# A fused two-layer block: biases in feature 0's row, three blocks of the Gram matrix, bank values' low parts beside the bank, and another opening order

## The reference, cut to what matters

```python
xn = layernorm(x)                                  # no scale, no shift
# layer 0, attention
q = xn @ Wq.T + bq;  k = xn @ Wk.T + bk;  v = xn @ Wv.T + bv
a = sigmoid(layernorm(q) @ layernorm(k).T / sqrt(D) - log(S))
s = ((a @ v) @ Wo.T + bo) * layerscale
# layer 0, feed-forward: 16 routed experts of 128, the top 4 of each row, and a shared one of 256
g = silu(routed(xn) + shared(xn))
x = x + s * g
xn = layernorm(x)
# layer 1, attention over a bank of 2048 keys K and values V
scores = xn @ K.T
s = gelu(scores / norm(scores, axis=-1) * sqrt(2048)) @ V
# layer 1, feed-forward with ternary weights, 1024 wide
g = silu(gelu(xn @ W1t.T + b1) @ W2t.T + b2)
return x + s * g
```

## Time and profile before

| What | us |
|---|---|
| Median of 3 runs (1258.23 to 1260.47) | 1259.47 |
| The profiled execution's own time | 1259.82 |
| Its span | 1256.6 |
| Busy: PE | 1213.6 (97%) |
| Busy: DVE | 892.8 (71%) |
| Busy: ACT | 555.5 (44%) |
| Busy: POOL | 426.0 (34%) |

### The profile page before, as it was taken

The page is one execution under the profiler, slowest core; times in us unless marked ns, Lnnn a source line. Parts: engine busy times, 40 slices in busy tenths (PEclk is TensorE's granted clock), DMA queues, the critical chain, the costliest instruction groups (busy, mean ns, idle before and its releaser), DMA issues.

```text
span 1256.6 us, 26657 instructions
## 1 busy us (share of the span) xinstructions
PE 1213.6 (97%) x8985; PEld 868.5 (69%) x8986; DVE 892.8 (71%) x1913; ACT 555.5 (44%) x1044; POOL 426.0 (34%) x391
## 2 busy tenths in 40 slices
PE   4899999999999999999999999999999999999998
PEld 3556667676688888866666667777766666666665
DVE  7897867565467766668899888999755455545554
ACT  6534643333266666656333334766632222222221
POOL 3332777776309180045777761231000000000000
PEclk9899999999999999999999999999999999999999
DMA  9898323333288666521566556442111011101100
GB/s 288 262 391 328 98 102 110 130 123 121 85 261 263 193 192 192 183 89 45 149 200 203 166 184 231 134 135 68 66 54 51 1 51 51 51 0 50 51 18 17
DMA packets 134063, 169.22 MB, mean 135 GB/s; under 512 B 12197, under 2 KB 121914, under 8 KB 131674
## 3 DMA queue, kind: packets, MB, share of 16 engines
q1 hardware_dynamic: 117386, 130.21, 31.7%
q0 software_dynamic: 12368, 33.70, 8.4%
q10 hardware_dynamic: 4224, 4.19, 1.0%
HBM read 84.18 MB, written 83.89 MB: 134 GB/s over the span
## 4 chain that ended last, share of the span: by engine, by line
PE 82%; DVE 7%; issue 5%; POOL 3%; ACT 2%; DMA 2%; SPq 0%; DVEq 0%; POOLq 0%; ACTq 0%
PE bank L1191 28%; PE sums L1238 24%; PE bank L1117 8%; PE sums L1205 5%; PE sums L1127 4%; PE bank L1097 3%; PE bank L1034 2%; PE sums L1366 2%; PE sums L1050 1%; POOL xg_d L821 1%; PE sums L1040 1%; DVE reg_e L2088 1%; PE sums L1069 1%; PE bank L1160 1%; PE bank L1059 1%
## 5 line engine op out<-in xcount | busy, mean ns | idle before, releaser
L2098 DVE TENSOR_SCALAR reg_w<-reg_w 128x512 f16<-128x512 f32 x320 | 146.8, 459 | 218.9 <-ACT reg_w L1590 218.5
L1238 PE MATMUL sums<-reg_v,reg_w 128*128 128x256 f16 x2304 | 282.4, 273 | 0.0
L1238 PEld LDWEIGHTS sums<-reg_v,reg_w 128*128 128x128 f16 x2304 | 225.4, 98 | 66.1
L1768 DVE SCALAR_TENSOR_TENSOR reg_w<-reg_w 128x512 f16<-128x512 f32 x320 | 223.1, 697 | 11.0
L1191 PE MATMUL bank<-reg_qk 128*128 128x512 f16 (+1 forms) x768 | 186.6, 379 | 0.0
L1191 PE MATMUL bank<-reg_qk,kbT 128*128 128x512 f16 (+1 forms) x768 | 186.6, 379 | 0.0
L1590 ACT ACTIVATE reg_w<-bank 128x512 f32<-128x512 f32 x128 | 76.5, 597 | 245.1 <-PE bank L1191 244.9
L1590 ACT ACTIVATE reg_w<-bank,nlogs 128x512 f32<-128x512 f32 x128 | 88.0, 688 | 179.2 <-PE bank L1191 172.8
L844 POOL DMA_INDIRECT reg_e<-yg_d,slot_i x128 | 131.0, 1023 | 46.5 <-issue 34.1
L839 POOL DMA_INDIRECT xg_d<-xr,icol x108 | 108.8, 1008 | 48.4 <-issue 26.4
L1191 PEld LDWEIGHTS bank<-reg_qk,kbT 128*128 128x128 f16 x768 | 75.1, 98 | 63.3
(11 more groups left out here) (242 smaller groups left out, 1739.8 us busy)
## 6 DMA issues: line engine op xcount, KB each, us to landing
xg_d<-kbT SPq DMA_DIRECT2D x18, 1024.0 KB, 5.5
xin<-xg_d SPq DMA_DIRECT2D x72, 256.0 KB, 2.8
yg_d<-xr SPq DMA_DIRECT2D x72, 256.0 KB, 2.2
reg_qk<-in_L_attn_x_dram SPq DMA_DIRECT2D x8, 512.0 KB, 8.2
sh_d<-xin SPq DMA_DIRECT2D x16, 256.0 KB, 3.2
xr<-xn_d SPq DMA_DIRECT2D x32, 128.0 KB, 2.1
reg_e<-sh_d SPq DMA_DIRECT2D x32, 128.0 KB, 2.7
moe_d<-reg_e SPq DMA_DIRECT2D x32, 128.0 KB, 2.0
```

The source lines that it names most:

```text
L1238: mm = pe.matmul(a_bank[2 * i + q // 2][:, (q % 2) * D:(q % 2 + 1) * D], part[:, j % 4, q * P:(q + 1) * P], m.second(y, j), start=(j == 0 ...
L1768: ins = dve.scalar_tensor_tensor(out=out_ap, in0=in_ap, scalar=scale, in1=hi_ap, op0=ALU.mult, op1=ALU.subtract)
L2098: dve.tensor_scalar(ah[:, j % 4, :], att[:, j % 2, :], m.split, None, ALU.mult).then_inc(m.hi_done, 1)
```

## The change

**Biases.** A normalized row has a feature mean of zero, so feature 0 is minus the sum of the others and can be left out of the product if each weight's column for feature 0 is subtracted from its other columns. `take_first` does that on DVE for Wq, Wk (four operations of 128 x 255 after x_moments(2)) and Wv (two, at chunk 3). Row 0 of `xT` is then free: POOL sets it to a constant (high part) and to 0 (low part) with `bias_row(b)`, once per batch, after the router and the shared expert have read it, and row 0 of the turned weights gets the biases (ACT `copy` 1x512 and DVE `low` 1x512 for q and k; for the value bv goes into Wv's column before it is turned). `project` loses its two bias matmuls; `biasz`, `ones_x`, `bias3`, the bias product of 6 matmuls in the opening and DVE's work on them go. PE waits for `less_first` before it turns Wq and Wk, and for `ones_row` at the first row tile of a batch.

**Openings.** SP starts x chunk 2 ahead of Wq and Wk, bv ahead of chunk 3, and chunk 3 ahead of the shared expert's weights. `ve` of the first layernorm moves from DVE to POOL. x_moments(3) stands ahead of chunk 0's low parts. In batch 0 ACT and DVE begin with the first two tiles without waiting for the end of the stage before, and ahead of the last rows to be stored.

**Scatters.** `beside` becomes 0 for tiles 0 to 3, then 2 and 1 in turn to tile 11, then 1: 16 rows beside the projection, 112 after it.

**Gram matrix.** `gram_part` now forms high·low for the whole matrix (32 matmuls of 256 columns) in one bank of sums, and high·high for the blocks (0,0), (1,0), (1,1) alone (16 x (128 + 256) columns) in another. Since low·high is the transpose of high·low, ACT copies the first out (`cross_m`) and PE adds it and its transpose with an identity times 16 (`ident_m`, which ACT writes): 5 matmuls, 768 columns. The block off the diagonal is doubled in the copies, each of which becomes two operations. `gram_products` multiplies half k = 1 with 256 columns and half k = 0 with 128. On ACT norm_x1(1) moves ahead of the last `sigmoid_step` and of the store's landing (its rows lie in `xr` now), the table load goes behind the new copy. PE turns the next rows ahead of `ff_mix`. POOL's gated(2) waits for the low parts of the first rows (`q4["l1"]`), and DVE's gate ahead of `ff_mix` goes.

**Bank values.** `bank_hi` and `bank_lo` of chunks 0 and 1 stay in `ff_mix` (at c = 6 and 7); those of the other six go into the first chunk of `bk_mix`, and PE waits there for the low parts of the value tiles that it is about to use.

```diff
@@ opening, SP
             load(st_rw, a["L0_ffn_router_weight"], "rw")
+            load_x_all(2)
             load(st_wq, rows(a["L0_attn_Wq"]), "qk")
...
             load(st_wv, rows(a["L0_attn_Wv"]), "o_v")
-            load_x_all(2)
+            load(bvf[:, :], a["L0_attn_bv"].rearrange("(t p) -> p t", p=P), "vb", allow_slow_non_contiguous=True)
+            load_x_all(3)
             load(st_sg, rows(a["L0_ffn_sh_gate_w"]), "sh")
@@ POOL
+                pool.tensor_scalar(ve[:, i, :], mv[:, i, :, 1], EPS, None, ALU.add).then_inc(ln["ve"], 1)
                 pool.wait_ge(ln["ve"], at(c))
...
+            def bias_row(b):
+
+                pool.wait_ge(rt_mm, NCH)
+                pool.wait_ge(shx["gu"], at(SX // B * (b + 1) - 1))
+                for h in range(2):
+                    pool.memset(xT[h][0:1, 0, b * S:(b + 1) * S], 0.0 if h else X_S).then_inc(ones_row, 1)
+            by(pool, SX, 4, shared_lo, pauses={SX // B: lambda: bias_row(0)})
...
-            beside = [0, 0] + [1 if t < 4 or t % 2 else 2 for t in range(2, S // P)]
+            beside = [0] * 4 + [2 - t % 2 if t < 12 else 1 for t in range(4, S // P)]
...
+            pool.wait_ge(q4["l1"], at(1))
             gated(2)
@@ PE, project
-                pe.matmul(s_bank[i % 4][:, :], ones_x[:, :], biasz[:, 0:2 * D], start=True, stop=False)
+                if isinstance(t, int) and t == 0:
+                    pe.wait_ge(ones_row, 2 * b + 2)
...
-                pe.matmul(v_ps, ones_x[:, :], biasz[:, 2 * D:3 * D], start=True, stop=False)
@@ PE, gram_products
-                for n, (k, (x, y)) in enumerate([(k, p) for k in range(KC) for p in THREE]):
-                    mm = pe.matmul(a_bank[2 * (1 - i) + t // 2][:, (t % 2) * D:(t % 2 + 1) * D],
-                                   xT[x][:, k, c * CW + t * P:c * CW + (t + 1) * P], gram[y][:, k, :],
-                                   start=(n == 0), stop=(n == 5))
+                for n, (k, (x, y)) in enumerate([(k, p) for k in (1, 0) for p in THREE]):
+                    ps = a_bank[2 * (1 - i) + t // 2][:, (t % 2) * D:(t % 2 + 1) * D]
+                    mm = pe.matmul(ps[:, gram_cols[k]], xT[x][:, k, c * CW + t * P:c * CW + (t + 1) * P],
+                                   gram[y][:, k, gram_cols[k]], start=(n == 0), stop=(n == 5),
+                                   skip_group_check=True)
@@ PE, the bank's first sums
-                    pe.wait_ge(vb_lo, NCH)
@@ PE, gram_part
-            def gram_part(row_tiles, begin, end):
+            def gram_part(ps, y, row_tiles, begin, end):
                 for k in range(KC):
-                    seq = [(m, p) for m in row_tiles for p in THREE]
-                    for n, (m, (x, y)) in enumerate(seq):
-                        mm = pe.matmul(a_bank[k][:, 0:D], kn[x][m // KN][:, m % KN, k * P:(k + 1) * P],
-                                       kn[y][m // KN][:, m % KN, :], start=(begin and n == 0),
-                                       stop=(end and n == len(seq) - 1))
+                    cols = slice(0, D) if y else gram_cols[k]
+                    for n, m in enumerate(row_tiles):
+                        mm = pe.matmul(ps[:, k, cols], kn[0][m // KN][:, m % KN, k * P:(k + 1) * P],
+                                       kn[y][m // KN][:, m % KN, cols], start=(begin and k == 0 and n == 0),
+                                       stop=(end and k == KC - 1 and n == len(row_tiles) - 1), skip_group_check=True)
                 return mm
...
+            gram_part(cross_ps, 1, others, False, True).then_inc(gram_mm, 1)
+            gram_part(gram_ps, 0, others, False, False)
+            pe.wait_ge(gram_hi, 1)
+            for k in range(KC):
+                pe.matmul(gram_ps[:, k, gram_cols[k]], ident_m[:, :], cross_m[:, k, gram_cols[k]], start=False,
+                          stop=False, skip_group_check=True)
+                for n in range(k + 1):
+                    mm = pe.matmul(gram_ps[:, k, n * P:(n + 1) * P], cross_m[:, n, k * P:(k + 1) * P], ident_m[:, :],
+                                   start=False, stop=(k == KC - 1 and n == KC - 1), skip_group_check=True)
+            mm.then_inc(gram_mm, 1)
...
+            turn_x(1, 0, s_bank[3])
...
+            def values_ready(j):
+                pe.wait_ge(vb_lo, j // VB_N + 1)
@@ ACT
-                elif j == 5:
-                    bank_hi(c)
+                elif j == 5 and c >= NCH - 2:
+                    bank_hi(c - (NCH - 2))
...
+            norm_x1(1)
             sigmoid_step(S // CW, 2)
+            act.activation(ident_m[:, :], ident[:, :], ACT.Copy, scale=MIX_S)
+            act.wait_ge(gram_mm, 1)
+            copy(cross_m[:, :, :], cross_ps, 1.0 / MIX_S, gram_hi)
             act.activation(thr[:, 0:1], onesf[:, 0:1], ACT.Gelu)
-            act.wait_ge(at_mix[1].stored[1], at_mix[1].st(S // CW // 2))
-            norm_x1(1)
...
             def last_queries_hi(c, j):
+                if first_step(c) and j < NCH - 2:
+                    bank_hi(j + 2)
@@ DVE
             x_moments(0)
-            x_moments(1, lambda: shifts(0, 0, ln, 2))
-            shifts(1, 1, ln, 2)
-            x_moments(2)
+            for c in range(1, 3):
+                x_moments(c, lambda: shifts(c - 1, (c - 1) % 2, ln, 2))
+            dve.wait_ge(ld["qk"], 16 * 2)
+            for w in (st_wq, st_wk):
+                take_first(w).then_inc(less_first, 1)
+            x_moments(3)
...
+                if b == 0:
+
+                    dve.wait_ge(shx["lo"], at(SX - 1))
+                    dve.wait_ge(shx["dn"], at(2 * (NCH - 2) + 1))
+                else:
+                    gate(dve, before)
                     gate(dve, end_late)
...
             def last_queries_lo(c, j):
+                if first_step(c) and 2 <= j < NCH:
+                    bank_lo(j)
```

167 lines of the change are left out of this document (84 added, 83 removed).

## The result

The changed kernel takes 1247.98 us in the median of six executions (1242.1 to 1249.45), the kernel before 1259.11 beside it (1257.63 to 1260.47): a ratio of 0.990, with an interval of 0.9875 to 0.9925. In a second measurement it took 1244.33 (1242.43 to 1245.44, five executions) against 1258.01 (1256.29 to 1262.93), 0.9883 (0.9866 to 0.990). So it is faster by 11 to 14 us, and the forecast was 18.1.

A forecast was written before the change was run, and what follows sets the result against it. PE was taken as the bound by its busy share, with the releaser deciding where PE waits. Gains of 0.8 + 0 + 4.4 + 4.1 + 3.6 + 5.2 = 18.1 us off 1259.82 gave 1241.7, 1241.4 on the median's footing; range 1236 to 1247.

The forecast's parts named there:

- likeliest case: Whole kernel: saved PE work is time where PE is full, elsewhere the releaser decides; 18.1 us less, 1241.4; chance 0.57.
- three signs by which it would have been wrong as a whole: Batch 1 DVE waits above 0.1 us a tile; first slots setting the pace; PE clock under 0.9 behind 44 us.
- Opening, shared expert: Opening: x chunk 2's wait goes, four subtractions come, gain 0.8 us; shared expert: 0, from -0.7 to +0.7.
- Rival 5: Granted clock stays low from the opening into the shared expert: slower, 1270 for half the stage, 1305 for all; chance 0.04.
- I take 0: Shared expert's stage: DVE's bias work goes, POOL's two memsets are hidden; no change, from -0.7 to +0.7 us.
- Projections, batch 0: Last tile turned 5.7 us earlier: 1.8 at the start, 0.7 for tiles 2 and 3, 3.2 for the last tiles.
- The scatter's tail: After batch 0's projection: 112 scatters at 1.53 us need 170.9; PE waits 1.3 at the first slots, 0 to 3.
- rival 2: Scatter's end binds: rows cost 1.6 us or start 3 later, PE waits 4.5 at the first slots; 1244.6; chance 0.12.
- Projections, batch 1: No scatters; PE's tile falls to 2.38 us, DVE at 2.44 to 2.49 is next: 4.1 less, from 3.3 to 5.0.
- Gram stage: PE work falls 4.1 us; waits of 0.9 and 0.65 replace 1.05: 3.6 less, between 0.5 and 4.5.
- Rival 4: Gram stage: the round trip through copy, table load and low part leaves 0.5 us instead of 3.6; 1244.5; chance 0.07.
- Products: Feed-forward: 96 matmuls at 128 instead of 256 columns save 0.054 us each, 5.2 less, DVE staying behind; 2.7 to 5.4.

The follow-up runs named there:

- first profile: Profile of one execution of the unaltered changed kernel, from the slower group of its first measurement: 1249.45 us.
- e8: Kernel before with the new scatter table alone: median 1330.20 us on another, slower chip; projection of batch 0 51.18 instead of 53.84.
- e1: Changed kernel with the old scatter table (20 rows beside the projection, from tile 2): 1248.71 us, 0.9919 of the kernel before.
- r2_after: Changed kernel, unaltered, run again on a third chip beside the kernels that alter POOL's scatter: 1299.69 us.
- r0_after: Changed kernel, unaltered, run again: 1244.33 us.
- e6: Changed kernel plus matmuls doing the removed bias matmuls' work: median 1327.61 us on another, slower chip; projections 49.90 (batch 0) and 47.15 (batch 1).
- first set: Follow-up runs on one chip, comparable by time: changed kernel again (1244.33), old table (1248.71), repeated router matmuls (1243.70), earlier DVE shifts (1242.32 us).
- e5: Changed kernel with products back at full width (output not the reference's): median 1323.82 us on another, slower chip; feed-forward 139.60.
- e3: Changed kernel with DVE's shifts for the next chunk's rows at feed-forward slice 5 instead of 6: 1242.32 us, feed-forward 135.43 instead of 137.27.
- e4: Changed kernel with all eight bank-value high and low parts back in the feed-forward: median 1327.40 us on another, slower chip; feed-forward 137.27.
- e11: Changed kernel with POOL's index copy made one group of four scatters ahead: 1429.59 us against 1299.69 for the changed kernel on the same chip.

## Why the forecast was right, and where not

**Direction and mechanism.** The likeliest case said that PE's saved work is time where PE is full, and POOL or DVE take the rest; it is so, and the time is 11 to 14 us lower. The forecast of 18.1 was too large by 4 to 7. Of the three signs by which it would have been wrong as a whole two came up: the first slots set the pace, and the granted clock was under 0.9 behind 44 us (0.78 at 44 to 48 and 0.66 at 340 to 344 in the first profile). The third, waits for DVE above 0.1 us a tile in batch 1, was at its edge (0.09 in the mean of eleven tiles, 0.12 in the last eight). The direction stands all the same; the two prices are in the paragraphs below.

**Opening, shared expert.** -0.8 was put down, and -0.7 and -0.9 came out up to the first projection. That is luck: two errors cancel, and both ends vary by execution. The opening itself gained 2.5 and 1.9: DVE's four subtractions took 1.10 us, not 1.4, and x chunk 2 was there without a wait (for chunk 3 DVE now waits 0.60). But 1.3 of that may be no work of the change, since e8, with the old opening, was through it at 42.77 and not at 44.06, and e1, with the new one, at 43.93. The shared expert's stage then gave back 1.8 and 1.0 at the lower clock. Where the clock stayed up in the unaltered kernel (r2_after), the first projection came at 109.48, 2.6 earlier than before. Rival 5 had named this mechanism and the place, with a stay of tens of us; it lasted about 4, and it also comes with the old opening (e8: stage 69.49). The step that failed is "I take 0" for this stage.

**Projections, batch 0.** -5.7 forecast, -5.2 and -5.4 measured. The wait at the scatters in tiles 4 to 11 is there (0.54 to 0.91 at every second tile). The parts are right in size for the last tiles (3.2 forecast; the table gave 2.7), and what e1 added, the first scatter in front of which POOL would stand 6.5 us, I had not seen. It did no harm to the forecast here, as it speaks for the new table.

**The scatter's tail.** A wait of 1.3 us at the first slots was forecast, within 0 to 3, and rival 2 had 4.5. The five profiles give 0.67 to 4.73. The step that failed is "164.8 us for 108, so 1.53 each": a value of one execution, in which 3 issues were slow, taken as a constant of the kernel. From the first index copy to the last scatter the 112 took 170.4 us in r0_after, as forecast (170.9), and 174.5 in the first profile. Rival 2 is what happened in the first profile. That it makes the two groups of times is not shown: the executions of e1, whose profile has no such wait, still span 5.9 us. Also not counted: behind the wait of 4.73 the clock falls (0.66 at 340 to 344 us in the first profile; 12 matmuls of 256 columns take 2.67 where r0_after has 1.47), and behind e6's of 3.83 too (0.57). It does not fall behind the waits up to 2.34, and yet the routed experts took 1.2 longer in r0_after and 0.3 to 1.0 in the other profiles of the first set, for which no run gives a cause.

**Projections, batch 1.** -4.1 forecast, -3.7 measured. In the first profile the first tiles come at PE's own 2.39 and from 557.35 on at 2.45 to 2.56, 2.48 in the mean of eleven (550.18 to 577.44); the forecast had 2.46 for all. From the first tile's products to the last's the gain is 3.9 (39.37 to 35.49). Behind them comes a tail to the last turning, for which the forecast added 0.1, and it became 0.16 longer (7.78 to 7.94). The lower end was also added up wrongly: 16 x 0.22 is 3.5 and not 3.3.

**Gram stage.** -3.6 forecast, -3.8 measured. The waits were smaller than taken:

```profile
765.25 0.23 PE L1436 MATMUL sums<-wpT,before_h 128*128 128x128 f16 x1 [0.43 <-ACT wpT L1459]
...
768.97 1.05 PE L1255 MATMUL sums<-w2T,reg_w 128*128 128x256 f16 x8 [0.19 <-DVE reg_w L1811]
```

0.43 and 0.19 instead of 0.9 and 0.65. Rival 4 is out. (The cover of the copy is 24 of the 48 later matmuls, not 32; the 2 us put on it are right for 24.) The old stage took 16.30 in e8 instead of 15.16; the new one took 11.3 to 11.4 in every profile.

**Products.** -5.2 forecast, -2.3 measured, the largest error in a stage that does not vary. The price of a matmul was right (e5), and so was the count. The step that failed is "DVE has 123.94 of 140 there and is next; ... so it stays behind". I judged by the busy share of an engine where a chain through three engines decides, with 0.97 of DVE's own idle time in it. With e3 1.8 of the missing 2.9 came back, and with the low part of e4 at slice 7 the stage did not change.

**What lay around the span.** The kernel before had 3.2 us between its time and its span in the profile, every other one 1.65 to 1.8, e8 among them, which is the kernel before but for a table. So 1.5 us of the difference between the profiled executions is not in any stage. I took the profiled execution as the basis and could not see this from one. The unprofiled executions say more: most of the kernel before also have 1.7 to 1.8, but 12 of its 55 in the three sets, and 2 of e8's ten, have 1.9 to 2.9, while none of the changed kernel and its variants exceeds 1.81. So it goes with the old opening or what else these two share; what it is stays open.

## What to carry to other kernels

Where a change takes cover away from a wait (8.9 us between the scatter's end and the turning before, 3.8 in r0_after and none in the first profile, of which the transfer needs 4.4), the length of what is covered must be known as a spread over executions, not as a value of one; under 8.9 us that spread had no effect, under 4.4 it has. An engine's busy share does not say that it has room: walk the chain of the slice that comes last, ACT to DVE to PE, and add its waits. And a stage's price holds at one granted clock: the same block took 10.5 to 12.6 us by the clock of that execution, with the old opening as with the new, so compare it at equal clock before a gain or a loss is booked.

## What the runs showed of the hardware

Beside POOL's indirect DMAs in closer order, 5.15 us for four (212 to 227 us in e11) instead of 5.86 (167 to 173 in the first profile), PE, ACT and DVE all but stood still, which made the kernel 130 us slower on one chip, at about the same traffic. I had taken POOL's waits for the copies as pure loss.

Some DVE operations beside a large operation on POOL last until POOL's ends: in e3 DVE's shifts of 128x4 elements, which have two operands, took 2.31 instead of 0.15, beside POOL's 2.35.

```profile
791.09 2.31 DVE L1884 SCALAR_TENSOR_TENSOR nmr<-mv,rstd 128x4 f32<-128x4 f32 x1 [0.17 <-POOL rstd L935]
...
791.03 2.35 POOL L946 TENSOR_TENSOR reg_e<-reg_e 128x1024 f32<-128x1024 f32 x1
```

They start within 0.06 us and end within 0.02. It goes with DVE's 3.33 of the earlier trace rows, and it is behind e3's remaining wait of 0.39 in the first chunk: there the shifts took 2.14 at 774.58, beside POOL's 2.34, and the low part that W2 waited for at 778.53 started at 777.78, behind two products for the norms and a TENSOR_SCALAR. The Trainium skill, page "SBUF — State Buffer", section "SBUF: two separate sides", says that the two share a pair of ports, that whoever starts first holds it for the whole instruction, and that DVE with two inputs in SBUF is concerned when POOL reads SBUF; these rows agree. An operation with one tensor operand is held as well: DVE's TENSOR_SCALAR of 128x512 (f32 to f16), 0.42 elsewhere, took 2.14 at 796.20 in the first profile, beside POOL's 2.35 from 795.71, and ended 0.28 behind it.

The gain of e3 was won in spite of it, since in the other chunks 2.31 us at slice 5 still end ahead of ACT's rows.
